# Summing the conditioning slices of the first attention on VectorE instead of GpSimd

## The chip, the core and the metric

One core of a Trainium2 chip runs the whole program. The time is device microseconds (us) of one execution. The profile shows five engines: TensorE (PE; its weight loads PEld), VectorE (DVE), ScalarE (ACT), GpSimd (POOL) and SyncE (SP), which here issues most DMA transfers. Each engine runs its own instructions in order and meets the others through semaphores.

## What is computed

Two layers on x of shape (4, 256, 256): conditioning and an attention, conditioning and a mixture of experts, twice. The conditioning is a two-sided scan along time, done once for each of the four places it is used and each of the four batches, 16 slices in all:

```python
_, (nf, df) = lax.scan(step, init, (ekv_t, ek_t))
_, (nb, db) = lax.scan(step, init, (ekv_t, ek_t), reverse=True)
num = nf + nb - ekv + euk * vf
den = df + db - ek + euk
base = jax.nn.sigmoid(r) * (num / jnp.maximum(den, 1e-08))
```

`x = x + attention0(conditioning(x, ...))` is the stage that this document is about. Its attention has 16 heads of width 16 with projections that mix the heads before and after the softmax.

## The kernel before

All of x lies in SBUF, transposed. The scans depend only on inputs, not on x, so their slices are put into gaps of other work. A slice (`slice_steps(n, nth, ...)`, a list of closures) is one use and one batch: `shifted` (the argument of the exponential), two forward scans into `num` and `den`, two backward scans into `backn` and `backd`, `own_term` (the product `euv`), then the sum of the terms, `floor` (the maximum with 1e-8), four quarter reciprocals `invert(0)` to `invert(3)`, and `finish` (the product into `fac`). Buffers `num`, `den`, `backn`, `backd`, `euk`, `euv` exist once, [128, 512] in float32 when flattened, so slices follow one another strictly.

Slice 0 is done first, with additions shared between VectorE and GpSimd. The first attention then runs over four batches b. Batch b works on slice 2b+1 (`own`) within its head loop, and begins slice 2b+2 (`split`) in its tail; the next batch ends that one. The order of VectorE's instructions in one batch is written out by hand:

- projections, stacks and the copies `turned`; then the copy of the first rank product (`rankq`, L1052), steps 6 to 8 of `split` (`floor`, `invert(0)`, `invert(1)`), the copy `rankkT` (L1056), two diagonals (`diagonals_pre`, L1086), and `invert(2)` and `invert(3)`. TensorE may begin the scores of the first pair of heads only after L1056 on VectorE and after L579 on ScalarE, the copy of the other half.
- the head loop over pairs p: `first_rank` (L1069), `maximum` (L1078), `mix` (L1102), `diagonals_pre`, reciprocals of row sums (L1107). Steps of `own` stand at the ends of iterations: the scans at p = 0 to 4, `own_term` (L929) at p = 5, `floor` with `invert(0)` and `invert(1)` at p = 7. At p = 8 come the other two inversions, `finish`, `condition_batch` (the next batch's input `xc`), and the last two `mix`.
- the tail: TensorE transposes the mixed queries (L1768, which waits for the last `mix`) and the mixed keys (L1774), transposes the head outputs (L1779), multiplies them out; VectorE copies `mixqT` (L1151), runs steps 0 to 3 of `split`, combines `o_tok` (L1158 to L1173), and then runs steps 4 and 5. TensorE meanwhile computes the next batch's hidden projection and then transposes `o_tok` (L1801, after L1173).

`own_term` raises `sums_in`. GpSimd waits for it in `sum_slice`, does four additions (L456, L457, L460, L461) and raises `sums_out`, for which `floor` waits. Slices 1 to 8 go that way, so there are 32 such GpSimd additions. Slice 8 is the last `split`: its `floor` falls in the shared expert's unit u = 6 (L1271 is the VectorE instruction of a unit). Slices 9 to 15 (`early`) are summed on VectorE, during the first mixture of experts, with three additions (L920, L921, L923) after the one of `early_own_term`.

`st(ins)` counts an instruction on the engine's own semaphore, `settle()` waits for the last counted one, `tell` raises a named semaphore instead.

Of the kernel before, what the change touches and what calls it, by code (L numbers as in the profile page):

```python
# [15 lines left out]
ALU = mybir.AluOpType  # L16
# [70 lines left out]
def build(nc, d, out, slots0, made0, slots, split1):  # L87
    ctx = ExitStack()
    with ctx:
# [10 lines left out]
        kT, ek, ekv = (side[:, n * CT * NT:(n + 1) * CT * NT].rearrange("p (c t) -> p c t", c=CT) for n in range(3))  # L100
        euk, euv, num, den, backn, backd = (sb(n, CT, T) for n in ("euk", "euv", "num", "den", "backn", "backd"))
# [142 lines left out]
        sums_in, sums_out = sem("cond_sums_in"), sem("cond_sums_out")  # L244
# [201 lines left out]
        def _(pool):  # L446
            st = Steps(pool, pool_own)
# [2 lines left out]
            st.settle()  # L450
            st.settle()

            def sum_slice(n, early=False):

                pool.wait_ge(sums_in, n + 1)
                st(pool.tensor_tensor(den[:], den[:], backd[:], ALU.add))  # L456
                st(pool.tensor_tensor(num[:], num[:], backn[:], ALU.add))  # L457
                st.settle()
                if not early:
                    st(pool.tensor_tensor(den[:], den[:], euk[:], ALU.add))  # L460
                st.tell(pool.tensor_tensor(num[:], num[:], euv[:], ALU.add), sums_out, n + 1)  # L461

            pool.wait_ge(sums_in, 1)
            st(pool.tensor_tensor(num[:], num[:], backn[:], ALU.add))
            st.settle()
# [2 lines left out]
            for b in range(B):  # L468
                pool.wait_ge(norm_in, b + 1)
                pool.tensor_tensor(ms, ms, spread(small[:, 40:42], 1, TT * 4), ALU.pow).then_inc(norm_out, 1)  # L470
                for n in range(2):
                    sum_slice(2 * b + 1 + n)


            pool.wait_ge(blank0, 16 * (E0 + 1))
# [22 lines left out]
            for buf in range(2):  # L498
                pool.memset(kst[:, buf, :, :, 24:25], 1.0)
                ins = pool.memset(vals1[:, buf, :, :, 8:9], 1.0)  # L500
# [354 lines left out]
        def _(dve):  # L855
            st = Steps(dve, dve_own)
# [22 lines left out]
            def slice_steps(n, nth, early=False, first=False):  # L879
# [4 lines left out]
                i, b = divmod(n, B)  # L884
# [41 lines left out]
                def own_term():  # L926
                    dve.wait_ge(*done["scan"])
                    dve.wait_ge(euk_out, nth + 1)
                    st.tell(dve.tensor_tensor(euv[:], euk[:], kT[:, :, cols], ALU.mult), sums_in, nth + 1)  # L929

                def first_sums():
                    dve.wait_ge(*done["scan"])
# [4 lines left out]

                def floor():
                    if not early and not first:
                        dve.wait_ge(sums_out, nth + 1)  # L940
                    st(dve.tensor_scalar(den[:], den[:], 1e-8, None, ALU.max))
                    done["floor"] = st.last

# [1369 lines left out]
```

## Time and profile before

| | |
|---|---|
| time, median of 3 runs | 1179.03 us (1178.47 to 1188.34) |
| the profiled execution's own time | 1185.53 us |
| its span, first to last instruction | 1183.7 us |
| TensorE busy | 983.3 us (83%) |
| VectorE busy | 800.8 us (68%) |
| ScalarE busy | 583.7 us (49%) |
| GpSimd busy | 210.9 us (18%) |
| mean granted TensorE clock | 0.943 |

The first attention takes about the stretch from 27 to 500 us of the span. Its batches repeat with a period of 116.3 us: `own_term` of batch 0 releases GpSimd at 109.3 us, that of batch 1 at 225.6, of batch 2 at 341.9 and of batch 3 at 458.1. Batch 1 is the one shown here.

In a timeline, a row is one instruction, or a run of like ones (xN), with its start, its length, engine, line, operation, output and inputs, shapes, and in brackets how long the engine had been idle before it and what ended that. Starts of instructions that follow closely on one engine lie nearer together than their lengths say, because they overlap in the pipeline. A granted clock of 1.00 is 2.4 GHz, 0.50 is 1.2 GHz.

### The profile page before, as it was taken

Reading aid. Unit: us, or ns where it says so; the run is one execution under the profiler, and the core shown is the slowest. Engines: PE = TensorE matmul, PEld = TensorE weight load, DVE = VectorE, ACT = ScalarE, POOL = GpSimd, SP = SyncE. Lnnn points to the kernel's source line nnn. Section 1 sums busy time; section 2 is a strip of 40 time slices with the busy share of each in tenths; the row PEclk is TensorE's granted clock in tenths of the full one; section 3 lists DMA queues with packets and bytes.
Section 4 is the critical chain, followed back from the end, with each engine's and each line's share of the span. In section 5 each row is a group of like instructions: output and inputs, shape, how many; then the busy total and the mean of one; then the engine's idle time right before and its main releaser. Section 6 shows DMA issues by size and latency. Waiting matters only on the chain.

```text
span 1183.7 us, 18440 instructions
## 1 busy us (share of the span) xinstructions
PE 983.3 (83%) x6324; PEld 704.1 (59%) x6324; DVE 800.8 (68%) x2060; ACT 583.7 (49%) x1444; POOL 210.9 (18%) x175
## 2 busy tenths in 40 slices
PE   1889888988899788698688898888898964999995
PEld 0667666766677677463466666623332453998884
DVE  6578878888788878763088887467667751554542
ACT  2388628853884488321333332236566722554442
POOL 1001020101011101127133333100000031232323
PEclk9999999999999999979799999979999985999998
DMA  9999400000000000024278884615454538577772
GB/s 261 257 231 246 112 1 1 1 1 1 1 1 1 1 2 1 28 95 164 95 233 273 282 272 152 213 71 189 168 213 172 189 119 310 170 234 214 223 226 27
DMA packets 75277, 161.30 MB, mean 136 GB/s; under 512 B 10658, under 2 KB 57262, under 8 KB 70960
## 3 DMA queue, kind: packets, MB, share of 16 engines
q1 hardware_dynamic: 66304, 145.52, 39.4%
q0 software_dynamic: 8880, 14.60, 4.8%
q8 instruction: 51, 0.84, 0.3%
q14 instruction: 42, 0.34, 0.1%
HBM read 127.68 MB, written 62.62 MB: 161 GB/s over the span
## 4 chain that ended last, share of the span: by engine, by line
PE 50%; DVE 15%; DMA 15%; ACT 9%; issue 5%; POOL 2%; another core or an unknown queue 2%; SPq 1%; ACTq 0%; POOLq 0%; DVEq 0%
PE ps L1629 46%; DMA out<-arena 7%; DMA arena<-in_w0all 4%; DMA made<-arena 3%; DVE arena L1416 2%; POOL out L519 1%; ACT arena L620 1%; ACT arena L605 1%; DVE arena L1078 1%; DVE arena L1040 1%; ACT arena L613 1%; PE ps L1729 1%; ACT arena L598 1%; DVE arena L1102 1%
## 5 line engine op out<-in xcount | busy, mean ns | idle before, releaser
L1629 PE MATMUL ps<-arena 128*128 128x256 f16 (+15 forms) x4712 | 776.4, 341 | 71.7 <-ACT arena L613 19.6
L1629 PEld LDWEIGHTS ps<-arena 128*128 128x128 f32 (+7 forms) x4712 | 533.1, 149 | 244.7 <-issue 98.8
L1613 DVE CAST arena<-arena 128x256 f16<-128x256 f32 x120 | 37.3, 311 | 99.7 <-ACT arena L827 98.9
L1416 DVE TENSOR_REDUCE arena<-ps 128x4 f16<-128x1024 f32 (+1 forms) x48 | 58.8, 1228 | 49.8 <-PE ps L1629 49.7
L1102 DVE SCALAR_TENSOR_TENSOR arena<-arena 128x128 f32<-128x128 f32 x240 | 84.0, 411 | 0.7 <-issue 0.3
L827 ACT ACTIVATE arena<-ps,arena 128x256 f32<-128x256 f32 x120 | 55.7, 474 | 58.2 <-PE ps L1629 55.5
L456 POOL TENSOR_TENSOR den<-den,backd 128x512 f32<-128x512 f32 x8 | 10.2, 1269 | 400.8 <-DVE euv L929 400.8
L620 ACT ACTIVATE arena<-ident,arena 128x128 f32<-128x128 f32 x256 | 81.0, 390 | 0.0
L488 POOL DMA_INDIRECT made<-arena x47 | 53.1, 1129 | 118.6 <-DVE arena L1329 117.6
L519 POOL DMA_INDIRECT out<-arena x30 | 47.6, 1587 | 145.4 <-DMA out<-arena 83.7
L1069 DVE SCALAR_TENSOR_TENSOR arena<-arena,ps 128x128 f32<-128x128 f32 (+1 forms) x128 | 47.2, 410 | 37.7 <-PE ps L1629 31.5
L735 ACT ACTIVATE arena<-ps 128x1024 f32<-128x1024 f32 x48 | 49.2, 1025 | 42.9 <-PE ps L1629 42.9
L948 DVE RECIPROCAL den<-den 128x128 f32<-128x128 f32 x64 | 56.5, 922 | 0.4
L1615 DVE TENSOR_TENSOR arena<-arena 128x256 f16<-128x256 f32 x120 | 51.1, 426 | 4.1
L508 POOL DMA_INDIRECT slots<-side x16 | 15.4, 964 | 214.3 <-DVE side L1502 210.0
L605 ACT ACTIVATE arena<-arena 128x128 f32<-128x128 f32 (+1 forms) x128 | 50.3, 440 | 0.0
L598 ACT ACTIVATE arena<-arena 128x128 f32<-128x128 f32 (+1 forms) x128 | 47.2, 440 | 0.0
L1629 PE MATMUL ps<-causal,identb 128*128 128x256 bf16 x160 | 36.2, 309 | 12.3 <-DVE arena L1416 9.7
L1078 DVE CUSTOM_DVE_ANT_0 arena<-arena 128x128 f32<-128x128 f32 (+1 forms) x128 | 46.2, 397 | 0.0
L1446 DVE TENSOR_TENSOR arena<-arena 128x512 f16<-128x512 f32 x64 | 42.4, 683 | 4.9 <-ACT arena L775 4.9
L703 ACT ACTIVATE arena<-ps 128x176 f32<-128x176 f32 x47 | 15.0, 318 | 62.1 <-PE ps L1629 60.1
L1086 DVE TENSOR_TENSOR arena<-ident,arena 128x512 f32<-128x512 f32 x64 | 44.5, 700 | 0.1
(283 smaller groups left out, 1251.5 us busy)
## 6 DMA issues: line engine op xcount, KB each, us to landing
arena<-split SPq DMA_DIRECT2D x15, 2048.0 KB
arena<-in_w0all SPq DMA_DIRECT2D x47, 608.0 KB
slots<-in_blank SPq DMA_DIRECT2D x17, 1040.0 KB, 15.5
arena<-in_w1all SPq DMA_DIRECT2D x16, 1024.0 KB, 6.6
split<-arena SPq DMA_DIRECT2D x32, 512.0 KB, 3.3
slots<-in_blank SPq DMA_DIRECT2D x9, 1072.0 KB, 17.8
arena<-slots SPq DMA_DIRECT2D x47, 130.0 KB, 3.0
side<-made SPq DMA_DIRECT2D x8, 512.0 KB, 5.8
```

Source lines behind the costliest of these rows:

```text
L488: pool.indirect_dma_start(made0[:], bass.IndirectOffsetOnAxis(ap=ids, axis=0), y0[:, j % Y0N], None, bounds_check=K0 * NT - 1, oob_is_err= ...
L519: pool.indirect_dma_start(out[:], bass.IndirectOffsetOnAxis(ap=ids, axis=0), ytok[:, j % 2, half], None, compute_op=ALU.add).then_inc(adde ...
L598: ins = act.activation(second[:, n % 2, cols], rankq[:, 1, cols], ACT.Copy, scale=mixw[:, tt, 0, 3, n:n + 1])
L605: ins = act.activation(prob[:, n % 3, cols], prob[:, n % 3, cols], ACT.Copy, scale=rinv[:, n % 2, tt:tt + 1])
L620: ins = act.activation(diag_post[:, n % 4, 2 * tt + i], ident[:], ACT.Copy, scale=mixw[:, tt, 3, i, n:n + 1])
L827: act.activation(hfull[:, m], ps[:, m, 0:SLOTS], ACT.Gelu, bias=bias[:, j % 3, 4 * layer + m:4 * layer + m + 1]).then_inc(l_read, 1)
L948: st(dve.reciprocal(part, part))
L1078: ins = dve.tensor_tensor_reduce(logit[:, s, tiles[tt]], logit[:, s, tiles[tt]], second[:, s, tiles[tt]], -1.0, 3.0e38, ALU.add, ALU.min, ...
L1102: ins = dve.scalar_tensor_tensor(dst, prob[:, n % 3, tiles[tt]], w, dst, ALU.mult, ALU.add)
L1416: dve.tensor_reduce(out, ps[:, at:at + 2].rearrange("p j (r s) -> p j r s", r=nr), X, ALU.max, negate=True).then_inc(max1_done, 1)
L1615: st.tell(dve.tensor_tensor(dst[:, 1, m], hfull[:, m], dst[:, 0, m], ALU.subtract), h_split, c + m + 1)
L1629: return pe.matmul(o, l, r, start=start, stop=stop, skip_group_check=shared)
```

## The change

`sum_slice` is removed from GpSimd. VectorE does the four additions of slices 1 to 8 itself, at the head of `floor`, in the order den and num, a wait for the second, den and num, a wait for the second. `own_term` no longer raises `sums_in`, except for slice 0, which stays as it was. GpSimd keeps the two additions of slice 0 and the power of each batch (L470).

```diff
--- before.py
+++ after.py
@@ -450,16 +450,6 @@
             st.settle()
             st.settle()
 
-            def sum_slice(n, early=False):
-
-                pool.wait_ge(sums_in, n + 1)
-                st(pool.tensor_tensor(den[:], den[:], backd[:], ALU.add))
-                st(pool.tensor_tensor(num[:], num[:], backn[:], ALU.add))
-                st.settle()
-                if not early:
-                    st(pool.tensor_tensor(den[:], den[:], euk[:], ALU.add))
-                st.tell(pool.tensor_tensor(num[:], num[:], euv[:], ALU.add), sums_out, n + 1)
-
             pool.wait_ge(sums_in, 1)
             st(pool.tensor_tensor(num[:], num[:], backn[:], ALU.add))
             st.settle()
@@ -468,8 +458,6 @@
             for b in range(B):
                 pool.wait_ge(norm_in, b + 1)
                 pool.tensor_tensor(ms, ms, spread(small[:, 40:42], 1, TT * 4), ALU.pow).then_inc(norm_out, 1)
-                for n in range(2):
-                    sum_slice(2 * b + 1 + n)
 
 
             pool.wait_ge(blank0, 16 * (E0 + 1))
@@ -926,7 +914,11 @@
                 def own_term():
                     dve.wait_ge(*done["scan"])
                     dve.wait_ge(euk_out, nth + 1)
-                    st.tell(dve.tensor_tensor(euv[:], euk[:], kT[:, :, cols], ALU.mult), sums_in, nth + 1)
+                    ins = dve.tensor_tensor(euv[:], euk[:], kT[:, :, cols], ALU.mult)
+                    if first:
+                        st.tell(ins, sums_in, 1)
+                    else:
+                        st(ins)
 
                 def first_sums():
                     dve.wait_ge(*done["scan"])
@@ -937,7 +929,12 @@
 
                 def floor():
                     if not early and not first:
-                        dve.wait_ge(sums_out, nth + 1)
+                        st(dve.tensor_tensor(den[:], den[:], backd[:], ALU.add))
+                        st(dve.tensor_tensor(num[:], num[:], backn[:], ALU.add))
+                        st.settle()
+                        st(dve.tensor_tensor(den[:], den[:], euk[:], ALU.add))
+                        st(dve.tensor_tensor(num[:], num[:], euv[:], ALU.add))
+                        st.settle()
                     st(dve.tensor_scalar(den[:], den[:], 1e-8, None, ALU.max))
                     done["floor"] = st.last
```

In the listings that follow, a row is an instruction in program order; 128x512 is its output's shape. Line numbers of the changed file are lower by 3 or by 12 than those of the file before. This is VectorE in batch 1 at the end of the iteration p = 7 and the start of p = 8. Before:

```order
L1107 RECIPROCAL arena<-arena 128x2
L941 TENSOR_SCALAR den<-den 128x512
L948 RECIPROCAL den<-den 128x128 x4
L955 SCALAR_TENSOR_TENSOR fac<-num,oscale,den 128x2x256
L977 SCALAR_TENSOR_TENSOR xc<-sig,fac 128x512
```

In the changed kernel, the same place:

```order
L1104 RECIPROCAL arena<-arena 128x2
L932 TENSOR_TENSOR den<-den,backd 128x512
L933 TENSOR_TENSOR num<-num,backn 128x512
L935 TENSOR_TENSOR den<-den,euk 128x512
L936 TENSOR_TENSOR num<-num,euv 128x512
L938 TENSOR_SCALAR den<-den 128x512
L945 RECIPROCAL den<-den 128x128 x4
L952 SCALAR_TENSOR_TENSOR fac<-num,oscale,den 128x2x256
L974 SCALAR_TENSOR_TENSOR xc<-sig,fac 128x512
```

Four additions stand between the row sums' reciprocal and the floor; the last eight `mix` instructions come after all of it. The second place is VectorE between the two rank copies, ahead of the head loop. Before:

```order
L1045 TENSOR_TENSOR arena<-arena 128x512
L1052 COPY arena<-ps 128x384
L941 TENSOR_SCALAR den<-den 128x512
L948 RECIPROCAL den<-den 128x128 x2
L1056 COPY arena<-ps 128x384
```

In the changed kernel, the same place:

```order
L1042 TENSOR_TENSOR arena<-arena 128x512
L1049 COPY arena<-ps 128x384
L932 TENSOR_TENSOR den<-den,backd 128x512
L933 TENSOR_TENSOR num<-num,backn 128x512
L935 TENSOR_TENSOR den<-den,euk 128x512
L936 TENSOR_TENSOR num<-num,euv 128x512
L938 TENSOR_SCALAR den<-den 128x512
L945 RECIPROCAL den<-den 128x128 x2
L1053 COPY arena<-ps 128x384
```

The copy for which TensorE waits now has four more instructions in front of it.

## Rows read from the trace of the kernel before

**Rows 1.** The page: chain that ended last by engine; a group of instructions.

```profile
PE 50%; DVE 15%; DMA 15%; ACT 9%; issue 5%; POOL 2%; another core or an unknown queue 2%; SPq 1%; ACTq 0%; POOLq 0%; DVEq 0%
...
L456 POOL TENSOR_TENSOR den<-den,backd 128x512 f32<-128x512 f32 x8 | 10.2, 1269 | 400.8 <-DVE euv L929 400.8
```

**Rows 2.** Timeline, VectorE, two head pairs of batch 1 (start us, us, line, shapes, idle).

```profile
218.21 0.74 DVE L1069 SCALAR_TENSOR_TENSOR arena<-arena,ps 128x128 f32<-128x128 f32 x2 [0.85 <-PE ps L1629]
...
220.47 0.42 DVE L1078 CUSTOM_DVE_ANT_0 arena<-arena 128x256 f32<-128x256 f32 x1
...
220.81 1.40 DVE L1102 SCALAR_TENSOR_TENSOR arena<-arena 128x128 f32<-128x128 f32 x4
...
226.99 0.74 DVE L1069 SCALAR_TENSOR_TENSOR arena<-arena,ps 128x128 f32<-128x128 f32 x2 [1.43 <-PE ps L1629]
...
229.90 1.48 DVE L1078 CUSTOM_DVE_ANT_0 arena<-arena 128x256 f32<-128x256 f32 x1
...
231.32 1.40 DVE L1102 SCALAR_TENSOR_TENSOR arena<-arena 128x128 f32<-128x128 f32 x4
```

**Rows 3.** Timeline, GpSimd, 225 to 235 us.

```profile
229.78 1.32 POOL L461 TENSOR_TENSOR num<-num,euv 128x512 f32<-128x512 f32 x1
```

**Rows 4.** Timeline, VectorE, end of the head loop and tail, batch 1.

```profile
241.42 0.17 DVE L1107 RECIPROCAL arena<-arena 128x2 f32<-128x2 f32 x1 [1.09 <-ACT arena L591]
...
242.90 0.41 DVE L941 TENSOR_SCALAR den<-den 128x512 f32<-128x512 f32 x1
...
248.16 2.91 DVE L1102 SCALAR_TENSOR_TENSOR arena<-arena 128x128 f32<-128x128 f32 x8
...
261.44 0.75 DVE L1173 TENSOR_TENSOR arena<-arena,ps 128x256 f32<-128x256 f32 x2
```

**Rows 5.** Timeline, TensorE, the same end and tail, batch 1.

```profile
238.28 0.55 PE L1729 MATMUL ps<-ident,arena 128*128 128x128 f32 x3 [0.88 <-ACT arena L605]
...
246.00 5.23 PE L1629 MATMUL ps<-arena 128*32 128x256 f32 x20 [0.58 <-ACT arena L613]
...
254.04 5.34 PE L1629 MATMUL ps<-arena 128*128 128x256 f32 x24
...
262.67 0.60 PE L1801 MATMUL ps<-ident,arena 128*128 128x128 f32 x4
```

**Rows 6.** Timeline, TensorE, end and tail of batch 3.

```profile
478.45 3.63 PE L1629 MATMUL ps<-arena 128*32 128x256 f32 x20 [0.58 <-ACT arena L613]
482.97 0.88 PE L1768 MATMUL ps<-ident,arena 128*128 128x128 f32 x6 [0.89 <-DVE arena L1102]
...
485.21 5.34 PE L1629 MATMUL ps<-arena 128*128 128x256 f32 x24
493.92 0.66 PE L1801 MATMUL ps<-ident,arena 128*128 128x128 f32 x4 [3.37 <-DVE arena L1173]
```

**Rows 7.** Timeline, VectorE, additions of a later slice.

```profile
600.96 0.68 DVE L920 TENSOR_TENSOR den<-den,backd 128x512 f32<-128x512 f32 x1
601.56 0.68 DVE L921 TENSOR_TENSOR num<-num,backn 128x512 f32<-128x512 f32 x1
602.28 0.69 DVE L923 TENSOR_TENSOR num<-num,euv 128x512 f32<-128x512 f32 x1
```

**Rows 8.** Timeline, all engines, start of batch 1's head loop.

```profile
170.03 0.49 DVE L1056 COPY arena<-ps 128x384 f32<-128x384 f32 x1
...
170.89 0.49 ACT L579 ACTIVATE arena<-ps 128x384 f32<-128x384 f32 x1 [2.13 <-PE ps L1629]
...
171.44 0.92 PE L1629 MATMUL ps<-arena 32*128 32x128 f32 x8 [0.58 <-ACT arena L579]
```

**Rows 9.** Windows of 2 us (bounds, sum, busy of engines, granted clock, DMA, GB/s).

```profile
246.00:248.00 2.00, 2.00 (x9) 1.05 (x10) 1.93 (x3) 1.11 (x4) 0.00 (x0) 0.50 0.00 0
```

**Rows 10.** Timeline, VectorE, the unit that follows slice 8's floor.

```profile
545.88 0.69 DVE L1271 TENSOR_TENSOR arena<-ps,arena 128x512 f32<-128x512 f32 x1 [1.74 <-ACT arena L677]
```

**Rows 11.** Timeline, ScalarE, 568 to 570 us.

```profile
569.62 0.59 ACT L677 ACTIVATE arena<-ps 64x512 f32<-64x512 f32 x1 [12.09 <-remote]
```

## The prediction

> **What bounds the kernel now.** I first read the page. The chain that ended last is half TensorE, and VectorE has 15% of it [rows 1], so work added to VectorE counts only where VectorE is the engine waited for. The additions that move are a small group, 8 times 1269 ns for one of the four lines [rows 1]. Four such additions take GpSimd about 5.1 us a slice, and it has nothing else to do then. So the question is what else happens at three places: where GpSimd adds now, and the two places at which VectorE will add. The timelines of batch 1 answer it.
>
> Where GpSimd adds now, in the head loop, TensorE sets the pace. From the start of `first_rank` to the start of `mix`, VectorE takes 220.81 - 218.21 = 2.60 us in an undisturbed pair, and 231.32 - 226.99 = 4.33 us in the pair that meets GpSimd's additions [rows 2]. The 256-wide `maximum` alone takes 1.48 us instead of 0.42 [rows 2]. So GpSimd's work is not free today: VectorE loses 1.73 us a batch to it. Instructions that read PSUM beside SBUF are not stretched (`first_rank` 0.74 in both), the ones with two SBUF inputs are.
>
> The stretched 256-wide instruction starts at 229.90 and GpSimd's last addition ends at 229.78 + 1.32 = 231.10 [rows 2, 3]. The Trainium skill (SBUF — State Buffer, "SBUF: two separate sides") says that a VectorE instruction with two SBUF inputs and a GpSimd instruction reading SBUF hold one port pair exclusively, each for its whole length. By that rule the instruction would take 1.20 + 0.42 = 1.62 us, the row says 1.48; taken for the whole price, the rule would give back 0.14 us more of VectorE's time a batch, 0.6 us in four, and I go by the row.
>
> **What is given back.** 1.73 us of VectorE's time, but not 1.73 us at the end. In the next pair VectorE waits for TensorE's scores anyway. What comes through does so by way of ScalarE: TensorE waited 0.88 us for its softmax at 238.28 [rows 5], and VectorE waited 1.09 us for its exponentials before the reciprocal at 241.42 [rows 4]. If ScalarE is that much earlier, VectorE gains at most the 1.09, since before it the engine was busy; TensorE gains about 0.9 or a little more. I take 1.0 us for both, with 0 and 1.09 as bounds.
>
> **What is added.** No row before has these four additions, but a later slice has three of the same shape: starts 600.96, 601.56 and, behind a wait for its predecessor, 602.28 [rows 7]. So one costs 0.60 us and one behind a wait 0.72. The new group has two of each (den, num, wait, den, num, wait): 2 x 0.60 + 2 x 0.72 = 2.64 us a slice. The wait for `sums_out` that goes was over long before: GpSimd ended at 231.10 and the floor starts at 242.90 [rows 3, 4]. Eight slices make 21.1 us of new VectorE work. They fall in three kinds of places.
>
> *The own slices (1, 3, 5, 7), end of the head loop.* From 241.42 to the end of the last `mix` at 248.16 + 2.91 = 251.07 VectorE never idles [rows 4]. TensorE's last values end at 246.00 + 5.23 = 251.23 and its transposes L1768 begin then, so neither has slack. With the additions the last `mix` ends at 251.07 - 1.0 + 2.64 = 252.71. Batch 3 shows the tail when VectorE releases it: L1768 at 482.97, the products at 485.21, 2.24 later [rows 6]. So batch 1's products start at about 252.75 + 2.24 = 254.99 instead of 254.04 [rows 5], 0.95 later. VectorE's own tail follows L1768 and moves by 1.64: `o_tok` is done at 261.44 + 0.75 + 1.64 = 263.83 instead of 262.19 [rows 4]. TensorE, which took up L1801 without waiting at the end of its products (262.67, the row's start overlapping what went before [rows 5]), comes there at about 263.7. The later of the two gives +1.0 us for the batch. In batches 0 to 2 this is 3 x 1.0. In batch 3 TensorE waited 3.37 us for VectorE at L1801 [rows 6], having no next batch to start, so VectorE's shift counts whole: 1.64. Sum 4.6 us.
>
> *The split slices (2, 4, 6), ahead of the next head loop.* TensorE starts the scores at 171.44, having waited for ScalarE's copy, which ended at 170.89 + 0.49 = 171.38. VectorE's copy L1056 ended at 170.03 + 0.49 = 170.52 [rows 8]. The slack is 0.86 us. VectorE is busy without a gap before that, so 2.64 us more bring L1056 to 173.16 and the scores to 173.20: +1.76. The diagonals that follow L1056 are ready in time; the first `first_rank` comes a little after its scores, but the second, which waits for TensorE, takes that up again. GpSimd's additions for these slices met only VectorE instructions that read PSUM, and give nothing back. Three batches: 5.3 us.
>
> *Slice 8.* Its floor stands in the shared expert's unit u = 6. Before the next unit VectorE idles 1.74 us, waiting for ScalarE [rows 10], and so again before later units, while TensorE may be up to three units ahead. The 2.64 us go into that idle time: 0. Without that cover they would cost 2.64.
>
> Sum of instruction times: 4.6 + 5.3 = 9.9 us.
>
> **TensorE's clock.** The first two microseconds of the last values in batch 1 ran at a granted 0.50, that is 1.2 GHz [rows 9]; the 20 matmuls took 5.23 us, and 3.63 us in batch 3 at 2.4 GHz [rows 5, 6], 1.60 us more. Before that drop TensorE had been mostly idle, waiting for ScalarE between short transposes. The changed kernel makes a longer hole: the last values end near 250.2, or 248.6 at the full clock, and L1768 starts at 252.75, so TensorE stands 2.5 to 4.1 us behind VectorE. I expect the clock to be low in the transposes and products behind it. Then the products end 1.60 us later still, VectorE's combination waits for them, and the batch ends 2.55 instead of 1.0 later; in batch 3 it is 2.55 instead of 1.64. If this happens in three of the four tails, it costs about 3 x 1.55 = 4.7 us (all four 5.6). The Trainium skill (TensorE: Matmul & The Clock Gate, "Part 1: The HAM clock gate") says the same of direction: idleness takes the clock to half, and where exactly it turns varies between runs. This is the rule that speaks most against the change.
>
> **The sum against the times.** 9.9 + 4.7 = 14.6 us. The span of 1183.7 lies 1.8 us inside its execution's 1185.53, and that execution was 6.5 us above the median of the runs, 1179.03. The change adds to either alike: 1183.7 becomes about 1198, and the median about 1193.
>
> **Rivals.**
> - *A (forecast), 0.52:* sums and low tails, 1179.0 + 14.6 = 1193.6, rounded to 1193. Its own range is 1189 to 1196.
> - *B, no further low clock, 0.20:* 1179.0 + 9.9 = 1188.9. For it: in batch 3 before, a similar sparse stretch left the clock at full speed (3.63 us for the same matmuls).
> - *C, the clock also falls at the start of the head loops, 0.15:* TensorE's wait there grows from 0.58 to 2.34 us. Three more times 1.60 make 1193.6 + 4.8 = 1198.4. Against it: the stretch ahead of it is dense.
> - *D, the additions are covered and the freed time comes through, faster than before, 0.05:* one mechanism, that TensorE and ScalarE are later than VectorE at both places. Then only the gain of 1.0 us a batch is left: 1179 - 4 = 1175. It decides if TensorE reaches L1768 more than 1.64 us after 251.07 and ScalarE's L579 ends later than 173.16. Both rows show less than 0.2 us of such cover in the first place and 0.86 in the second.
> - *E, a supply stall moves, 0.08:* ScalarE stood 12.09 us for something that is no engine of this program before its silu at 569.62 [rows 11], while TensorE had nothing to do. The later timetable, or VectorE's 32 more instructions, could remove it (1193.6 - 12.1 = 1181.5) or make another like it (1205.7). ScalarE's instructions are unchanged, which speaks against it.
>
> **How the numbers follow.** About 1% (11.8 us) is what a measurement of this kernel can tell from no change, so the bounds are 1167.2 and 1190.8. Slower by over 1%: nearly all of A, C, a part of B and E, 0.65. Within 1%: most of B, the low end of A, D and the lost stall of E, 0.32. Faster by more would need D and the lost stall together: 0.03. The range goes from 1184 to 1200: it holds A, B and C with the scatter of a median, and leaves out D and E, 0.13.
>
> **What would show it.** In the trace after: `maximum` at 0.42 us in every pair, and 2.60 us from `first_rank` to `mix` in the pair after `own_term`; the four additions 2.64 us from the first start to the floor; a wait of TensorE at L1768 for VectorE's `mix` in every batch; a wait of TensorE for the copy L1056 (now L1053) of about 2.3 us in batches 1 to 3; the batches' period at about 116.3 + 1.0 + 1.8 = 119.1 us, 120.7 with a low tail; the granted clock 0.50 behind the tail's wait. The prediction is wrong if the period grows by less than 2 us or by more than 6, or if stages after 500 us change their length.

## The result and the profile after

| | before | after |
|---|---|---|
| median of the runs timed side by side | 1181.15 us (1178.47 to 1188.34) | 1198.5 us (1191.16 to 1212.63) |
| ratio, 95% interval | | 1.0111 (1.0076 to 1.0146) |
| the profiled execution's own time | 1185.53 us | 1196.96 us |
| its span | 1183.7 us | 1194.0 us |
| VectorE busy | 800.8 us | 813.7 us |
| GpSimd busy | 210.9 us | 169.8 us |
| mean granted TensorE clock | 0.943 | 0.943 |

The kernel became slower, by 1.1%. The forecast was 1193.0 us with 1184 to 1200 around it; the ratio is worth 13.1 us on 1181.15, and the sum had said 14.6. The median of 1198.5 takes in one slow execution (1212.63 us) of four, which the ratio leaves out; the other three have 1196.96 in the middle.

The page gives the chain that ended last, by engine. VectorE's share has gone from 15% to 21%, TensorE's from 50% to 44% [rows 1]:

```profile
PE 44%; DVE 21%; DMA 16%; issue 8%; ACT 6%; POOL 2%; another core or an unknown queue 1%; SPq 1%; ACTq 0%; POOLq 0%; DVEq 0%
```

VectorE's timeline of the changed kernel, batch 1 and the start of batch 2 (start, length, line, operation, shapes, idle before it). Lines are 3 lower than in [rows 2, 4, 8].

```profile
228.04 0.74 DVE L1066 SCALAR_TENSOR_TENSOR arena<-arena,ps 128x128 f32<-128x128 f32 x2 [1.43 <-PE ps L1626]
...
230.30 0.42 DVE L1075 CUSTOM_DVE_ANT_0 arena<-arena 128x256 f32<-128x256 f32 x1
...
230.64 1.40 DVE L1099 SCALAR_TENSOR_TENSOR arena<-arena 128x128 f32<-128x128 f32 x4
...
241.41 0.17 DVE L1104 RECIPROCAL arena<-arena 128x2 f32<-128x2 f32 x1
...
242.89 0.67 DVE L932 TENSOR_TENSOR den<-den,backd 128x512 f32<-128x512 f32 x1
...
244.20 0.69 DVE L935 TENSOR_TENSOR den<-den,euk 128x512 f32<-128x512 f32 x1
...
245.52 0.43 DVE L938 TENSOR_SCALAR den<-den 128x512 f32<-128x512 f32 x1
...
286.38 0.68 DVE L932 TENSOR_TENSOR den<-den,backd 128x512 f32<-128x512 f32 x1
...
289.02 0.43 DVE L938 TENSOR_SCALAR den<-den 128x512 f32<-128x512 f32 x1
...
291.16 0.49 DVE L1053 COPY arena<-ps 128x384 f32<-128x384 f32 x1
```

Four things are to be seen. The pair after `own_term` takes 230.64 - 228.04 = 2.60 us and its wide `maximum` 0.42, where it was 4.33 and 1.48 [rows 2]. The reciprocal at 241.41 has no idle time in front of it any more, where it had 1.09 [rows 4]. The additions take 245.52 - 242.89 = 2.63 us in the tail and 289.02 - 286.38 = 2.64 ahead of the next head loop. And the copy that TensorE waits for starts as much later.

TensorE's timeline of the changed kernel at the same places, and in batch 3's tail:

```profile
246.13 5.27 PE L1626 MATMUL ps<-arena 128*32 128x256 f32 x20 [0.58 <-ACT arena L601]
253.77 0.87 PE L1765 MATMUL ps<-ident,arena 128*128 128x128 f32 x6 [2.36 <-DVE arena L1099]
...
256.00 5.35 PE L1626 MATMUL ps<-arena 128*128 128x256 f32 x24
...
276.74 6.25 PE L1681 MATMUL ps<-ident,arena 128*128 128x128 f32 x40 [1.86 <-DVE arena L1022]
...
291.80 0.92 PE L1626 MATMUL ps<-arena 32*128 32x128 f32 x8 [2.46 <-DVE arena L1053]
...
491.80 0.88 PE L1765 MATMUL ps<-ident,arena 128*128 128x128 f32 x6 [1.77 <-DVE arena L1099]
...
502.75 1.11 PE L1798 MATMUL ps<-ident,arena 128*128 128x128 f32 x4 [3.36 <-DVE arena L1170]
```

Both waits that the forecast named are there: 2.36 us at the transposes L1765 (was none in batch 1, 0.89 in batch 3 [rows 5, 6]; it is 1.77 now), and 2.46 us ahead of the scores (was 0.58, for ScalarE [rows 8]). A window of the changed kernel, 2 us behind the first of them (bounds; sum; busy of PE, PEld, DVE, ACT, POOL with counts; granted clock; DMA share, GB/s), shows what is not there:

```profile
254.00:256.00 2.00, 2.00 (x20) 2.00 (x19) 1.65 (x5) 0.94 (x3) 0.00 (x0) 1.00 0.00 0
```

The clock stayed at 1.00, that is 2.4 GHz, behind the tail's wait.

**One yardstick for all runs.** The experiments are compared by the stretch from the first transposes of the stacks in batch 0 (L1684 before, L1681 after) to the start of the last addition into x of the first attention (L990, L987). It is 456.90 us before (42.00 to 498.90) and 466.47 after (41.89 to 508.36): +9.57 of the 10.3 us by which the span grew. What follows it took 684.8 us before and 685.6 after. But between executions this rest varies from 668 to 689 us, whatever was done to the first attention (a second profile of the kernel before has 679.7, two more of the changed kernel 673.9 and 677.2), so a span or a single time can't resolve a few microseconds; the stretch leaves this rest out. Where the rest gets its scatter from is shown under "The stall E" below.

### The profile page after: what moved, and what is told of

It reads as the page before. It is cut to its first block, busy times and chain, and to the rows that moved or that the text cites. A ratio compares the mean times of both kernels' runs of the same rounds, so it can differ in the third digit from the quotient of the medians.

```text
span 1194.0 us, 18440 instructions
## 1 busy us (share of the span) xinstructions
PE 980.7 (82%) x6324; PEld 705.5 (59%) x6324; DVE 813.7 (68%) x2092; ACT 584.1 (49%) x1444; POOL 169.8 (14%) x143
## 4 chain that ended last, share of the span: by engine, by line
PE 44%; DVE 21%; DMA 16%; issue 8%; ACT 6%; POOL 2%; another core or an unknown queue 1%; SPq 1%; ACTq 0%; POOLq 0%; DVEq 0%
PE ps L1626 40%; DMA out<-arena 9%; DMA arena<-in_w0all 3%; DMA made<-arena 3%; DVE arena L1413 2%; POOL out L507 2%; DVE den L945 2%; DVE arena L1099 1%; ACT arena L601 1%; DVE arena L1037 1%; PE ps L1726 1%; ACT arena L608 1%; PE ps L2051 1%; DMA ident<-in_ident 1%
## 5 line engine op out<-in xcount | busy, mean ns | idle before, releaser
L460 POOL TENSOR_TENSOR arena<-arena,small 128x16 f32<-128x16 f32 x4 | 11.6, 2906 | 366.6 <-DVE arena L1008 366.6
L471 POOL DMA_INDIRECT slots<-arena x32 | 33.2, 1039 | 148.0 <-DVE arena L1262 138.6
## 6 DMA issues: line engine op xcount, KB each, us to landing
slots<-in_blank SPq DMA_DIRECT2D x9, 1072.0 KB, 18.9
```

## The experiments

In the diffs, which stand against the changed kernel, "..." leaves lines out. A *fall* is a place where the granted clock, read in steps of half a microsecond, goes under 1.00. Falls are counted from the start to the end of the stretch. The experiments ran on three chips, with medians of the kernel before of 1168.99, 1181.74 and 1183.13 us; ratios are taken on the same chip.

**The changed kernel again.** No edit, on the first chip.

> The changed kernel once more, beside the others of this chip. Theory T (instruction times alone, no further low clock): the end of the first attention, the last addition into xT before the mixture, comes 9.9 us later than before, so the time is 1.0084 of before. Rival K (TensorE's clock is low in the longer holes of the tails in many executions, though not in the profiled one): 14.6 us, 1.0124, with 0.50 granted behind the last mix of some batch in this profile.

Median 1189.14 us, ratio 1.0172 (1.0123 to 1.0222), stretch 472.97 us, so +16.3 over the mean of the two profiles of before, 456.7. TensorE's timeline of this execution in batch 0's tail, then two windows:

```profile
135.44 1.25 PE L1765 MATMUL ps<-ident,arena 128*128 128x128 f32 x6 [2.33 <-DVE arena L1099]
136.48 1.49 PE L1771 MATMUL ps<-ident,arena 128*128 128x128 f32 x6
137.76 1.75 PE L1776 MATMUL ps<-ident,arena 128*128 128x128 f32 x8
139.35 5.34 PE L1626 MATMUL ps<-arena 128*128 128x256 f32 x24
```

```profile
136.00:138.00 2.00, 2.00 (x12) 2.00 (x11) 1.83 (x5) 0.49 (x1) 0.00 (x0) 0.50 0.05 14
177.00:179.00 2.00, 2.00 (x12) 2.00 (x11) 1.53 (x3) 0.00 (x0) 0.00 (x0) 0.50 0.00 0
```

The same wait of 2.33 us is followed here by 1.2 GHz (0.50), and the transposes take 139.35 - 135.44 = 3.91 us; in the profile of after it was 2.23 in batch 1 (256.00 - 253.77). The second window lies in the first scores of batch 1: there the clock is low too. So one program gives different falls from execution to execution, and there are two places for them. Batch 1's tail in the same execution shows how a tail gets a longer wait:

```profile
250.27 3.63 PE L1626 MATMUL ps<-arena 128*32 128x256 f32 x20 [0.58 <-ACT arena L601]
257.91 0.87 PE L1765 MATMUL ps<-ident,arena 128*128 128x128 f32 x6 [4.01 <-DVE arena L1099]
259.83 1.92 PE L1776 MATMUL ps<-ident,arena 128*128 128x128 f32 x8
```

The last values ran at full clock (3.63 us, where batch 1 of the profile of after has 5.27), so TensorE was through earlier, and VectorE's last `mix` came no earlier: the wait is 4.01 instead of 2.36 us, and the clock falls behind it (the eight transposes L1776 take 1.92 us; 1.04 in the profile of after). A fall in the last values is hidden by the wait that the change makes, one in the tail is not.

**Each half alone.** Only the slices 1, 3, 5, 7 (`own`) summed on VectorE and the others on GpSimd as before, and the other way round:

```diff
                 def floor():
                     if not early and not first:
-                        st(dve.tensor_tensor(den[:], den[:], backd[:], ALU.add))
...
+                        if nth % 2 == 1:
+                            st(dve.tensor_tensor(den[:], den[:], backd[:], ALU.add))
...
+                        else:
+                            dve.wait_ge(sums_out, (nth + 1) // 2 + 1)
```

> Slices 1, 3, 5, 7 are summed on VectorE at floor, slices 2, 4, 6, 8 stay on GpSimd. T: 3 x 1.0 + 1.6 = 4.6 us over before (1.0039); the copy of rankkT keeps its 0.9 us of slack and TensorE waits for VectorE at the transposes of the mixed queries in every batch. K: up to 10 us, since all of the low clock belongs to these tails (1.0085).

> Slices 2, 4, 6, 8 are summed on VectorE at floor, slices 1, 3, 5, 7 stay on GpSimd. T: 3 x 1.8 = 5.3 us over before (1.0045), all of it a wait of TensorE for the copy of rankkT (about 2.4 us, three times); maximum still stretched to 1.48 us by GpSimd's additions. K: 5.3 too. If the split slices cost nothing, own_only must carry the whole change.

Own slices alone: 1.0077 (1.0039 to 1.0115), stretch 459.33 us, +2.6, with a fall in one tail, behind a wait of 4.01 us. Split slices alone (2, 4, 6, 8): 1.0124 (1.0068 to 1.0181), stretch 467.55, +10.8. The two ratios add up to 2.0%, against 1.7% for both together on that chip. In the first, the wait ahead of the scores stays as it was, and the tail has it; in the second, the tail keeps its length and the scores wait, TensorE's timeline of the split-only kernel:

```profile
172.70 0.92 PE L1641 MATMUL ps<-arena 32*128 32x128 f32 x8 [2.47 <-DVE arena L1068]
...
173.78 4.47 PE L1641 MATMUL ps<-arena 128*128 128x128 f32 x24
```

Behind that wait the clock fell at 174, 293.5 and 412.5 us, in all three batches; from the first transpose of the stacks to the first `first_rank` these took 18.67, 19.03 and 19.19 us, against 15.70 before and 17.84 in the profile of after, where there was no fall. In the traces the split half costs more than the own half, and part of that is a fall that the forecast thought unlikely. The two ratios have intervals that overlap, so the order of the halves in the timed runs is not shown.

**The same additions on VectorE, in its gaps.** All four additions of each slice stay on VectorE, but stand where it waits for TensorE: the two with the backward terms and the two with the own terms behind p = 5 and p = 6 for `own`, and all four in a row for `split`, behind the first scaled copies of the next batch (`scaled_qk`), ahead of `residual_first`.

```diff
+                def back_sums():
+                    dve.wait_ge(*done["scan"])
...
+                def own_sums():
+                    dve.wait_ge(*done["back"])
...
                 def floor():
                     if not early and not first:
-                        st(dve.tensor_tensor(den[:], den[:], backd[:], ALU.add))
...
+                        dve.wait_ge(*done["sums"])
...
                 if b:
+                    for step in split[12:14]:
+                        step()
                     residual_first(b - 1)
...
-                extra = {0: split[11:12] + own[0:1], 1: own[1:2], 2: own[2:3], 3: own[3:4], 4: own[4:5], 5: own[5:6],
-                         7: own[6:9]}
+                extra = {0: split[11:12] + own[0:1], 1: own[1:2], 2: own[2:3], 3: own[3:4], 4: own[4:5], 5: own[5:6] + own[12:13],
+                         6: own[13:14], 7: own[6:9]}
```

> All additions of slices 1 to 8 on VectorE, but in gaps of VectorE: for own slices two additions behind own_term (p = 5) and two at the end of p = 6, for split slices all four behind the next batch's first scaled copies, ahead of the residual. T (the place decides, and GpSimd's additions cost 1.0 us a batch before): 4 us faster than before (0.9965), stretched maximum gone, no wait of TensorE for the copy of rankkT above 0.6 us. Rival V (any 21 us more on VectorE cost about the same wherever they stand): about 10 us slower than before.

Median 1166.97 us, ratio 0.9981 (0.9955 to 1.0007), stretch 452.47, that is 4.2 us under before. VectorE's timeline of the gaps kernel behind p = 6 of batch 1:

```profile
229.34 0.69 DVE L931 TENSOR_TENSOR den<-den,euk 128x512 f32<-128x512 f32 x1
229.94 0.69 DVE L932 TENSOR_TENSOR num<-num,euv 128x512 f32<-128x512 f32 x1
231.45 0.74 DVE L1076 SCALAR_TENSOR_TENSOR arena<-arena,ps 128x128 f32<-128x128 f32 x2 [0.83 <-PE ps L1638]
```

and TensorE's in the tail of that batch:

```profile
245.81 0.82 PE L1777 MATMUL ps<-ident,arena 128*128 128x128 f32 x6
```

After the additions VectorE still has 0.83 us to wait for TensorE, and the transposes start without waiting for it. On one chip this kernel and the changed one differ only in where the same 32 instructions stand, and by 1189.14 - 1166.97 = 22.2 us (20.5 in the stretch). This decides against the rival that VectorE's work costs as such. The 22.2 us are those of one chip and hold the falls of the clock as well as the instruction times. What is left when the price of the place is gone is the return of GpSimd's port time: forecast 4 x 1.0, measured 4.2 in this trace; the ratio alone would not separate it from nothing.

**The lock by itself.** GpSimd does four additions of the same size on buffers that nobody uses, in the own slices, beside VectorE's real ones, and VectorE's floor waits for them.

```diff
+                pool.wait_ge(sums_in, b + 2)
+                st(pool.tensor_tensor(spare[0], spare[0], spare[2], ALU.add))
+                st(pool.tensor_tensor(spare[1], spare[1], spare[3], ALU.add))
...
```

> The changed kernel, and GpSimd still does four additions of the same form when own_term of slices 1, 3, 5, 7 is done, on memory that nobody uses. T (GpSimd's additions cost VectorE 1.7 us a batch, of which 1.0 reaches the end): maximum is stretched to about 1.48 us again and the time is 4 us above the changed kernel, since VectorE sets the end of the head loop. Rival: if the freed time never reached the end, the time is that of the changed kernel and only the idle time of VectorE shrinks.

Median 1201.71 us, ratio 1.0168 (1.0126 to 1.0210), stretch 482.65. VectorE's timeline of this kernel in batch 1:

```profile
233.21 1.05 DVE L1095 TENSOR_TENSOR arena<-ident,arena 128x512 f32<-128x512 f32 x1
...
235.48 1.49 DVE L1087 CUSTOM_DVE_ANT_0 arena<-arena 128x256 f32<-128x256 f32 x1
```

TensorE's timeline in the same batch's tail, then a row of its waits from 27 to 520 us (total, times, longest):

```profile
259.36 1.54 PE L1777 MATMUL ps<-ident,arena 128*128 128x128 f32 x6 [4.16 <-DVE arena L1111]
260.70 1.49 PE L1783 MATMUL ps<-ident,arena 128*128 128x128 f32 x6
261.98 1.91 PE L1788 MATMUL ps<-ident,arena 128*128 128x128 f32 x8
```

```profile
PE ps L1777 <- DVE arena L1111: 16.0, 4, 4.2
```

The stretched `maximum` is back at 1.49 us (1.48 in [rows 2]), with no data in common between the two engines, so the price is not one of waiting for results. That it is one of access to SBUF fits the rows, in which instructions that read PSUM are not stretched (`first_rank`, 0.74 us in both pairs of [rows 2]). From the first `first_rank` to the tail the batches 1 to 3 take 79.6, 79.6 and 79.0 us, about 1.1 more than in the profile of after (78.3, 78.5, 77.9). The tail's wait starts at the end of values that had run at full clock in this execution, and is 4.16 us long in this batch (3.56 to 4.16 in the four); behind it the clock was low in all four. The 4 us over the changed kernel that were expected of the time are not shown by the runs: the changed kernel was not timed on this chip, and its three ratios, 1.0091, 1.0111 and 1.0172, enclose this 1.0168. What is shown is the stretched instruction and the 1.1 us a batch in the trace. The Trainium skill (SBUF — State Buffer, "SBUF: two separate sides") describes this port pair as an exclusive lock. Taken at its word it would have a floor of 1.20 + 0.42 = 1.62 us for the row of 1.49; the rows fit the direction and fall 0.13 short of the figure.

**No additions at all.** The four additions of slices 1 to 8 are left out on both engines, so these slices' conditioning is another; a bound for what moving them can bring.

```diff
                     if not early and not first:
-                        st(dve.tensor_tensor(den[:], den[:], backd[:], ALU.add))
...
+                        dve.wait_ge(*done["own"])
```

> The additions of slices 1 to 8 are left out on both engines, so the conditioning there lacks its backward and own terms. T: 1.0 us a batch is given back by GpSimd's silence, 4 us below before (0.9965), and the end of the head loop has no wait of TensorE for VectorE above 1 us. Rival (GpSimd's additions were free before): 1.000.

Median 1181.91 us, ratio 0.9977 (0.9952 to 1.0001), stretch 455.43, with eight falls, two of them twice as long as the others. TensorE's timeline of this kernel in batch 1's tail:

```profile
248.33 0.88 PE L1761 MATMUL ps<-ident,arena 128*128 128x128 f32 x6 [1.35 <-DVE arena L1095]
```

The trace has a wait of TensorE for VectorE's last `mix` of 1.35 us in batches 1 and 2 (none above 1 was expected), behind values at full clock. The stretch is 1.3 us under before, not 4, with two falls twice as long; the ratio does not tell 0.9965 from 1.000.

With neither engine adding, the time is that of the gaps version (0.9981), where VectorE adds everything. So in a gap the additions are free within what can be measured, and the most that any placing of them could win is about 0.2%, 0.5% at the end of the interval.

**The waits filled.** If the clock term is real, useless matmuls in TensorE's new waits should take the falls away. 14 (then 10) products of the identity, into PSUM columns that nobody reads at that time, stand ahead of the tail's transposes and ahead of the scores.

```diff
+                for _ in range(10 if b else 0):
+                    mm(ps[:, 1, 384:512], ident[:], ident[:], True, True, True)
                 pe.wait_ge(evac_a, b * EVA0 + 13)
...
+                for _ in range(10):
+                    mm(ps[:, 1, 384:512], ident[:], ident[:], True, True, True)
                 pe.wait_ge(h_done, b * N0 + N0)
```

> The changed kernel with 14 short matmuls of no use (identity by identity, 128x128, into columns that nobody reads) put on TensorE into each of its two new holes: ahead of the wait for the last mix in every batch, and ahead of the wait for the copy of rankkT in batches 1 to 3. Nothing is taken off VectorE. Clock theory K (the change costs more than its instruction times, because the holes let the clock fall): the granted clock no longer falls behind these two places, and the time comes down to the instruction times alone, some 9 to 11 us above before (1.008 to 1.0095) where the changed kernel had 1.011 and 1.017. Rival M (the excess is elsewhere, in the mixtures' transfers, and the low clock is hidden): unchanged, 1.011 to 1.017, or a little slower.

> As fill_holes, with 10 matmuls of no use a hole instead of 14, so that they end before the wait does (14 took 3.3 us, the hole ahead of the scores is 2.5 us). K: no fall of the clock behind the two holes, and a time below that of the changed kernel beside it by 3 to 8 us. M: no difference to the changed kernel beside it.

> The changed kernel a third time, for the comparison with fill_holes10 on the same chip. T alone 1.0084 of before; with K 1.0124 (four or so falls of the clock in the new holes that are not hidden).

> The kernel before once more, to have its profile from this chip: the end of the first attention and the places where the granted clock falls (all theories: two falls in most batches' head loops, none behind a copy of rankkT or in a tail but the last).

| kernel, chip | median | ratio (95%) | stretch | falls of the clock, behind the two new waits |
|---|---|---|---|---|
| 14 matmuls, second chip | 1192.39 | 1.0094 (1.0060 to 1.0128) | 472.78 | 10, none |
| 10 matmuls, third chip | 1193.37 | 1.0087 (1.0055 to 1.0119) | 466.78 | 11, none |
| changed kernel, third chip | 1195.38 | 1.0091 (1.0062 to 1.0120) | 475.62 | 14, five |
| kernel before, second chip, one run | 1178.57 | | 456.47 | 7 |

Fourteen were too many. TensorE's timeline with 14 in batch 0's tail (a product counts as two instructions, so x28):

```profile
132.71 3.29 PE L1626 MATMUL ps<-ident 128*128 128x128 f32 x28
135.84 0.82 PE L1772 MATMUL ps<-ident,arena 128*128 128x128 f32 x6
```

and with 10:

```profile
130.96 2.39 PE L1626 MATMUL ps<-ident 128*128 128x128 f32 x20
133.55 0.87 PE L1769 MATMUL ps<-ident,arena 128*128 128x128 f32 x6 [0.19 <-DVE arena L1099]
```

3.29 us is longer than the wait that it fills (2.3 to 2.5 in most batches), so work that was ready stood behind it; with 2.39 us TensorE still waits 0.19. In the changed kernel beside it, on the third chip, the clock is low in three of the four tails and at two of the three starts of the scores. Batch 3 is one of these tails; its eight transposes take 1.04 us at full clock, and here:

```profile
498.60 0.87 PE L1765 MATMUL ps<-ident,arena 128*128 128x128 f32 x6 [3.41 <-DVE arena L1099]
...
499.99 1.92 PE L1776 MATMUL ps<-ident,arena 128*128 128x128 f32 x8
```

In the traces the fillers do what was expected: no fall behind either wait, and the ten have 466.78 us where the changed kernel on the same chip has 475.62. The 8.8 us between them are about the price of those five falls, at 1.65 us each. The timed runs don't confirm it: 1193.37 against 1195.38, with intervals that cover each other. That the falls stop is shown; that this wins several microseconds of the median is not.

**The clock held up through the head loops.** The gaps version, with fillers in several short waits of the first and the last pairs and ahead of the stacks' transposes.

```diff
+                for _ in range(6):
+                    mm(ps[:, 5, 384:512], ident[:], ident[:], True, True, True)
...
+                def filler(n, start):
+                    for _ in range(n):
+                        mm(ps[:, 6, 384:512], ident[:], ident[:], start, start, True)
...
+                    if n in (0, 1, 15):
+                        filler({0: 3, 1: 5, 15: 5}[n], n < 2)
...
+                    if p in (0, 7):
+                        filler(2, p == 0)
```

> The kernel with the additions in VectorE's gaps, and matmuls of no use on TensorE at the sparse start and end of each head loop (4, 8 and 3 around the first two transposed probabilities, 9 and 3 around the last). In the profile of gaps every batch has about two falls of the granted clock there, each with 1.7 us of work at half speed. K: most of these falls go, up to 8 x 1.6 = 13 us, of which some is hidden: 0.985 to 0.993 of before. M: no gain over gaps (0.998), or a loss, since the extra matmuls delay the real ones.

> The additions in VectorE's gaps, and matmuls of no use at the sparse places, sized to the idle time there (3, 5 and 2 at the start of the head loop, 5 and 2 at its end, 6 ahead of the stacks' transposes). Those that follow the first pair in bank 6 do not start an accumulation group. K (the granted clock at the sparse places is worth about 1.7 us each time it stays up): 0.985 to 0.992 of before, with fewer falls of the clock in the profile than the eight of gaps. M: 0.998 as gaps.

The first try (3 to 9 fillers at those places, all with the start flag) has ratio 0.9881 (0.9845 to 0.9917) and stretch 446.05. Its fillers also changed the sums of the attention (see the last section), so its time is that of the same instructions on other numbers. The second has 0.9919 (0.9892 to 0.9946) with median 1173.24 us and stretch 445.33. TensorE's timeline of the second at the start of batch 1's values, then its stretch from 60 to 475 us as one window:

```profile
176.20 0.55 PE L1746 MATMUL ps<-ident,arena 128*128 128x128 f32 x3
176.58 1.28 PE L1638 MATMUL ps<-ident 128*128 128x128 f32 x10
178.06 0.55 PE L1746 MATMUL ps<-ident,arena 128*128 128x128 f32 x3 [0.19 <-ACT arena L593]
...
179.19 4.49 PE L1638 MATMUL ps<-arena 128*32 128x256 f32 x28
```

```profile
60.00:475.00 415.00, 380.08 (x2635) 311.00 (x2634) 367.55 (x1067) 292.18 (x902) 8.70 (x3) 1.00 0.18 42
```

The granted clock of this window is 1.00, where it is 0.97 before (0.98 in its second profile) and in the gaps version, 0.96 after and 0.95 in the two repeats of after. No fall is left up to 480 us, and the stretch is 7.1 us under the gaps version's. This is the only version with unchanged results whose ratio is clear of 1.000 on the fast side; on its chip it is faster than the kernel before by 0.8% and than the changed one by 1.9% (1173.24 against 1183.13 and 1195.38).

## Why the forecast held, point by point

- **GpSimd's port time comes back, 1.0 us a batch.** Held. VectorE's pair fell from 4.33 to 2.60 us, the 1.09 us of idling before the reciprocal went, and from `first_rank` of p = 7 to the reciprocal 1.06 us is saved, in this batch. In the total it is less firm: the gaps kernel's stretch is 4.2 us under before, that of the kernel without additions 1.3, and neither ratio is clear of 1.000.
- **2.64 us of additions a slice.** Held: 2.63 and 2.64. The 5.1 us that the prediction has for the four additions on GpSimd come from one line's mean; in batch 1 they take 231.10 - 225.64 = 5.46, since the third of them is longer than the others:

```profile
228.22 1.60 POOL L460 TENSOR_TENSOR den<-den,euk 128x512 f32<-128x512 f32 x1
```

Nothing else in the sum uses the figure. The sum gives 1193.6, which would round to 1194; the forecast has 1193.

- **The tail, +1.0, +1.0, +1.0, +1.64.** By its instructions it held: against before, from the first `first_rank` to the transposes of `o_tok`, the batches differ by -0.70, +0.67, +0.94 and +1.47 us. Batch 0 lacks a fall that before had at 68.5 us; with its 1.65 us it is +0.95. The last batch has another +0.6 us behind it: the transposes that waited 3.36 us for VectorE run in 1.11 us instead of 0.66 [rows 6]. That wait existed before, and only its shift was counted. So 9.57 against 9.9 is near in part by luck: +1.1 ahead of the scores (next point) and +0.6 here against the 1.65 of the fall that batch 0 lacks.
- **Ahead of the scores, +1.76.** Mis-sized: it is +1.98 to the scores and +2.14 to the first `first_rank`, three times, so 6.4 instead of 5.3 us. The forecast let the second `first_rank` take up the delay of the first; both rank copies' followers on VectorE are late, and nothing takes it up. 0.1 us is another fall: the stack transposes of 276.74 ran in 6.25 us, 5.20 before, and all but 0.1 of that vanished in a wait behind them.
- **Slice 8, 0.** Nothing contradicts it. No run isolated it: after the stretch, 684.8 against 685.6 us, within what that rest varies anyway.
- **The order of the halves.** The forecast put 9.3 us with the clock on the own slices (4.6 + 4.7) and 5.3 on the split ones; measured alone they are 0.77% and 1.24% (9.0 and 14.5 us on 1168.99), 2.6 and 10.8 us in the stretch. The own half's ratio agrees with the forecast, its single trace does not; the split half is above 5.3 in both. A clock term was missing there, and whether the own half's was too large is not shown.
- **The period.** 119.15 and 119.30 us between the first `first_rank` of batch 1 and 2, and of 2 and 3; forecast 119.1, before 116.2.
- **The clock term, 4.7 us in three tails.** As a statement on one execution it failed: the profiled one had no fall in any tail, and came out as rival B, with +9.57 us against the sum of 9.9. As a statement on the kernel it held in size and not in place. The three traces of the changed kernel have +9.8, +16.3 and +18.9 us over 456.7, in the mean +15.0, against 14.6 forecast. The low tails were none, two and three of four, where the forecast had three; the other new falls came behind the scores' wait, none, one and two of three, and in three of three with the split half alone. An estimate from these rows: 11 us of instruction times (4.0 in the tails, 0.6 behind the last, 6.4 ahead of the scores) and 1.65 for each of none, three and five falls make 11, 16.0 and 19.3 us, against the measured 9.8 (where batch 0 has one fall less than before), 16.3 and 18.9. That the mean comes within half a microsecond of 14.6 is luck: an instruction term too small by 1.1 us, and 2.7 falls on average in two places where the forecast had three in one. This is rival C's mechanism, put aside because "the stretch ahead of it is dense"; that was the weakest sentence of the forecast, argued from one trace. A and C are not two cases but two places at which the same thing happens or does not. The length of the wait was forecast well: 2.5 to 4.1 us, with values at either clock, and the rows have 2.36 and 4.01.
- **The clock, at what wait.** Behind waits of 2.3 to 2.5 us at these two places the clock fell in some executions and not in others; behind the seven that were longer (4.01, 3.41 and 4.01 in the two repeats of the changed kernel and the own half alone, 3.56 to 4.16 in the four tails of the lock run) it fell each time. The Trainium skill (TensorE: Matmul & The Clock Gate, "Part 1: The HAM clock gate") says that idleness takes the clock to half and that the point varies between runs; the three traces of one program agree.
- **The stall E.** ScalarE's timeline of the changed kernel, around the silus of the shared expert:

```profile
571.01 0.59 ACT L665 ACTIVATE arena<-ps 64x512 f32<-64x512 f32 x1 [7.20 <-issue]
580.89 0.59 ACT L665 ACTIVATE arena<-ps 64x512 f32<-64x512 f32 x1 [9.30 <-remote]
```

In this pair of profiles it made no difference: the first addition into x of the next stage comes 9.2 us later (749.0 before, 758.2 after), as the stretch ended 9.5 later. But the stall is not a property of either kernel. The last silu in the second profile of the kernel before, then in the two repeats of the changed one:

```profile
564.01 0.59 ACT L677 ACTIVATE arena<-ps 64x512 f32<-64x512 f32 x1 [9.54 <-remote]
```

```profile
574.21 0.59 ACT L665 ACTIVATE arena<-ps 64x512 f32<-64x512 f32 x1 [2.84 <-PE ps L1626]
581.44 0.59 ACT L665 ACTIVATE arena<-ps 64x512 f32<-64x512 f32 x1 [7.71 <-remote]
```

In these five executions the wait is 12.09 and 9.54 us before, and 9.30 (with 7.20 ahead of it), 2.84 (for TensorE, as ahead of most silus, so no stall) and 7.71 after; what follows the stretch is 684.8, 679.7, 685.6, 673.9 and 677.2 us. So E's stall comes and goes with the execution, with or without the change, and most of the scatter of the rest goes with it. It is absent in all four traces of the first chip and 6.0 to 12.1 us long in the eight of the other two; the rest is 671 us on average there and 678 and 683 here, most of the 13 to 14 us between the chips' medians. Neither sign of E came true for the change. Why ScalarE stands there stays open.
- **What stays open** is the size of one fall's share in the median. The ratios of the changed kernel, 1.0111, 1.0172 and 1.0091, lie further apart than one interval, and the fillers, which removed falls in the trace, moved the median by 2 us only.

## What to carry to other kernels

Before work is moved to an engine, look for the instruction of it that another engine waits for, and put the work behind that one, not ahead of it: the same 32 additions, ahead of a copy and of the last `mix` for which TensorE waits, cost 22 us more than in VectorE's own waits on one chip (1189.14 against 1166.97), and 13 us more than leaving them out on another (1195.38 against 1181.91). Sum the instruction times against one trace, but treat TensorE's clock as a chance per wait and per execution: it needs two or three traces of one kernel, and one undisturbed trace hides it. A freed engine may give time back through a shared port, here about 1 us of GpSimd's 5.5 in each batch's rows.

## What the runs showed of the hardware that was not expected

- A fall of the clock doesn't need a sparse stretch before it. It came behind a single wait of 2.5 us at the scores, between dense work, in none, one and two of three batches of the changed kernel's three traces and in three of three with the split half alone, and costs 1.6 to 1.7 us each (in the tail, 3.91 against 2.23 us for the same 20 transposes).
- Useless matmuls in short waits pay for themselves here: 0.97 to 1.00 of granted clock over 415 us, 7.1 us in the stretch.
- A fall costs nothing where another wait hides it. From the start of the last values (20 matmuls) to the tail's first transpose the changed kernel took 7.64 us with a fall (246.13 to 253.77) and without (250.27 to 257.91).
- A filler in other columns of a PSUM bank isn't harmless. In the first try fillers with the start flag wrote columns 384 to 512 of the bank in whose columns 0 to 256 the values were being summed, and the attention's sums came out changed (0.07 relative). The version with the flag cleared at the places inside an open sum didn't do this; the two differ in the numbers of fillers too, so the cause is argued, not isolated. The Trainium skill (PSUM — Partial Sum Buffer, "The four PSUM rules") states the rule that fits: the first matmul of a sum clears the written marks of the whole bank, so that a sum open beside it starts over.
- The same kernel differs by as much between chips (1168.99 against 1183.13 us) as the change is worth. Only times of one chip can be compared.
